# First attention: both score matmuls interleaved in two halves of the TensorE array, and later keys zeroed after the exponential

## The chip, the cores and the metric

One core of one Trainium2 chip. The metric is the device time of one execution in microseconds (us), the median of three runs.

## The reference

Two layers run on a stream of 16 sequences of 256 tokens with 128 channels: attention, experts, a second attention with fixed offsets, and experts with a capacity. The change lies in the first attention:

```python
q = apply_rope(q) * scale          # (16, 16 heads, 256, 8)
k = apply_rope(k)
dots = jnp.einsum('bnih,bnjh->bnij', q, k)
i = jnp.arange(l)
mask = i[:, None] < i[None, :]
dots = jnp.where(mask, jnp.float32(-100000.0), dots)
attn = jax.nn.softmax(dots, axis=-1)
o = jnp.einsum('bnij,bnjh->bnih', attn, v)
return o.transpose(0, 2, 1, 3).reshape(b, l, d) @ Wo.T + bo
```

## The kernel before

`attention0` is a pipeline over the 16 batches. On every engine one function, `run`, takes a list of steps written by hand, each with a stage letter, and issues the list once per repeat b. The letter tells which batch the step works on: L is b+4 (layer norm), A b+3 (projections, rotation, split), S b+2 (values, last part, loads), M b+1 and N b+2 (maxima of the scores), C b (exponentials and outputs), D b−1 (division, projection out, residual). Every engine works through its own list strictly in order; semaphores tie them together.

Scores must be as exact as float32, but are computed from bfloat16 terms. GpSimd adds the two halves of the rotation (`split_parts`, L403) and splits the sum into three bfloat16 parts (L407, L409, L411 and, as `last_part`, L417). SP stores the parts to DRAM in six transfers (L364, L367) and loads them back (L370) with the six products of parts as 48 rows (8 channels by 6 terms) under `qs` and `ks`, for all heads. Both have three buffers, one per batch in flight.

From these TensorE computes the scores twice. `scores_m(g, n)` has queries on partitions and keys along the row; VectorE takes each row's maximum (`maxima`, L672). `scores_c(g, n)` has keys on partitions and queries along the row. Three further rows of `qs` there hold the negated maximum in three parts (L382, L384), so that ScalarE's exponential (`exps`, L437) needs nothing more. Heads go in four groups g, and each group in three units n: units 0 and 1 are two heads of 256 columns, unit 2 is four heads of 128. Each unit fills one PSUM bank: first a matmul of the identity with a mask (`causal`, L472), which puts −1e30 where the key is later than the query, then the score matmuls on top of it (L488, L495 for c; L513, L520 for m). `outputs(g)` multiplies the exponentials `pr` (two buffers, by g) with the values (L546, L548), once the group's three exponentials are done.

The steps that the prediction speaks of, in TensorE's list: `project(1)` (L568) gives the keys' projection of batch b+3, which `rotate(1)` on VectorE (L649, L651) turns and GpSimd splits; `scores_m(0, 0)` of stage N is the first use of batch b+2's loads, and waits for `spread`, the semaphore of both loads; `turn_normal` is L592, `turn_max` L532, `project_out` L598. `statistics` (L625 to L632) on VectorE precedes GpSimd's `rstd_of` (L395, L397), and `normalise` (L638) follows it.

GpSimd's list is short:

```python
run(pool, [("S", last_part), ("A", split_parts), ("L", rstd_of)])
```

## Time and profile before

| | us |
|---|---|
| median of 3 runs | 1368.03 |
| lowest, highest | 1363.39, 1371.96 |
| the profiled execution, its time | 1355.89 |
| its span in the trace | 1354.0 |
| first attention in the span | about 0 to 445 |
| TensorE, VectorE, ScalarE, GpSimd busy in the span | 82%, 60%, 36%, 22% |
| mean granted TensorE clock | 0.882 of full speed |

Full speed of TensorE's clock is 2.4 GHz and its lower level 1.2 GHz. Matmuls are pipelined, so what one costs is read from the distance of two starts, not from its duration. A row of several instructions (x4) is a merged stretch. An arrow in brackets names what an idle time ended with. VectorE is DVE, ScalarE ACT, GpSimd POOL, and SP issues all DMAs of this stage.

### The profile page before, as it was taken

The page shows a single profiled execution, that of the slowest core. Times are in us where ns is not written, and L with a number is a line of the kernel's source. Part 1 is how long each engine was busy: PE and PEld are TensorE (multiplying, and loading weights), DVE is VectorE, ACT ScalarE, POOL GpSimd, SP SyncE. Part 2 cuts the span into 40 slices and gives each one's busy share as a digit, 9 for nine tenths or more (in the row PEclk, how much of TensorE's full clock was granted, in tenths as well). Part 3 has the DMA queues.
Part 4 walks back from the last instruction along what each step waited for, and adds up shares of the span by engine and source line. Part 5 has one row for each costly group of instructions (what it writes and reads, how often), then busy time and mean ns, then how long its engine had stood idle before and what let it go on. Part 6 is the DMA issues. An engine that isn't in the chain of part 4 may idle for free. (4 is left out here: it accounts for less than half of the span.)

```text
span 1354.0 us, 25150 instructions
## 1 busy us (share of the span) xinstructions
PE 1105.7 (82%) x9345; PEld 654.5 (48%) x9345; DVE 815.0 (60%) x1910; ACT 483.5 (36%) x839; POOL 298.3 (22%) x283
## 2 busy tenths in 40 slices
PE   3699999999999599999999996588888889845140
PEld 2235454544444244444444442376777667744130
DVE  4456666646552466566666653488888888646322
ACT  0024444424445133323323321455555564411020
POOL 4132323213210000000000002342332321015536
PEclk9969999959999699999999998589999999855575
DMA  4534242422420622321332230323223322040233
GB/s 128 143 97 96 51 95 49 94 48 49 96 51 3 230 80 94 104 90 63 124 96 95 62 126 0 111 80 97 78 68 96 96 65 81 1 125 26 71 105 85
DMA packets 83989, 113.38 MB, mean 84 GB/s; under 512 B 9658, under 2 KB 53616, under 8 KB 81664
## 3 DMA queue, kind: packets, MB, share of 16 engines
q1 hardware_dynamic: 81840, 108.65, 28.5%
q0 software_dynamic: 2048, 3.37, 0.9%
q8 instruction: 64, 1.05, 0.3%
q14 instruction: 37, 0.30, 0.1%
HBM read 80.18 MB, written 32.65 MB: 83 GB/s over the span
## 5 line engine op out<-in xcount | busy, mean ns | idle before, releaser
L672 DVE TENSOR_REDUCE a_nmax<-ps 128x2 f32<-128x512 f32 (+1 forms) x192 | 132.4, 691 | 127.7 <-PE ps L513 88.2
L437 ACT ACTIVATE a_pr<-ps 128x512 f32<-128x512 f32 x192 | 114.2, 597 | 173.9 <-PE ps L488 124.9
L861 ACT ACTIVATE e_sg<-ps 128x512 f32<-128x512 f32 x136 | 81.2, 597 | 244.6 <-PE ps L886 231.5
L1050 DVE TENSOR_TENSOR e_up<-e_sg,ps 128x512 f32<-128x512 f32 x128 | 88.0, 687 | 106.9 <-PE ps L893 100.9
L886 PE MATMUL ps<-e_hT,e_wg 128*128 128x512 f32 x272 | 140.8, 600 | 0.8 <-DVE e_wT L1037 0.8
L902 PE MATMUL ps<-e_hm,e_wd 128*128 128x512 f32 x272 | 139.2, 594 | 1.4 <-DVE e_hm L1053 0.7
L472 PE MATMUL ps<-a_mask,identb 128*128 128x256 bf16 (+1 forms) x384 | 129.1, 336 | 13.5 <-DMA a_ks<-a_terms_d 9.4
L893 PE MATMUL ps<-e_hT,e_wu 128*128 128x512 f32 x272 | 139.8, 596 | 0.0
L1053 DVE TENSOR_TENSOR e_hm<-e_up,e_wb 128x512 f32<-128x512 f32 x128 | 88.5, 692 | 5.6
L902 PEld LDWEIGHTS ps<-e_hm,e_wd 128*128 128x128 f32 x272 | 51.5, 190 | 67.3 <-issue 63.5
L893 PEld LDWEIGHTS ps<-e_hT,e_wu 128*128 128x128 f32 x272 | 52.1, 191 | 65.6 <-issue 59.8
L1581 POOL TENSOR_TENSOR a_prod<-a_q,a_kp 128x768 f32<-128x768 f32 (+1 forms) x32 | 53.3, 1688 | 131.8 <-PE ps L1789 128.3
L886 PEld LDWEIGHTS ps<-e_hT,e_wg 128*128 128x128 f32 x272 | 50.0, 193 | 53.0 <-issue 51.7
L472 PEld LDWEIGHTS ps<-a_mask,identb 128*128 128x128 bf16 x384 | 38.1, 99 | 70.3 <-issue 38.4
L403 POOL TENSOR_TENSOR a_ra<-a_ra,a_rb 128x512 f32<-128x512 f32 x16 | 20.2, 1262 | 235.4 <-DVE a_rb L651 235.4
L837 POOL TENSOR_TENSOR e_rstd<-e_mv,eps 128x4 f32<-128x4 f32 x8 | 1.6, 199 | 290.2 <-DVE e_mv L964 290.2
L1861 DVE TENSOR_TENSOR a_lg<-ps,a_gw 128x1024 f32<-128x1024 f32 x32 | 59.0, 1886 | 9.9 <-PE ps L1768 8.3
L513 PE MATMUL ps<-a_ks,a_qs 48*128 48x256 bf16 x256 | 54.5, 297 | 0.0
L488 PE MATMUL ps<-a_qs,a_ks 51*128 51x256 bf16 x256 | 52.5, 287 | 0.0
L1882 DVE TENSOR_TENSOR a_lg<-a_lg,a_bias 128x2208 f32<-128x2208 f32 x16 | 49.3, 3079 | 2.1 <-DVE a_lg L1872 0.5
L1571 POOL TENSOR_TENSOR a_rstd<-a_mv,eps 128x2 f32<-128x2 f32 x16 | 30.7, 1920 | 72.9 <-DVE a_mv L1845 72.9
L1621 ACT ACTIVATE a_pT<-ps 128x512 f32<-128x512 f32 x64 | 34.4, 597 | 32.2 <-PE ps L1672 32.2
(266 smaller groups left out, 2031.6 us busy)
## 6 DMA issues: line engine op xcount, KB each, us to landing
e_wb<-e_wT_d SPq DMA_DIRECT2D x128, 256.0 KB, 3.3
a_gw<-a_gd_d SPq DMA_DIRECT2D x16, 1024.0 KB, 5.0
a_gd_d<-a_gc SPq DMA_DIRECT2D x64, 132.0 KB, 2.3
a_terms_d<-a_parts SPq DMA_DIRECT2D x32, 192.0 KB, 2.1
a_qs<-a_terms_d SPq DMA_DIRECT2D x16, 384.0 KB, 5.0
a_ks<-a_terms_d SPq DMA_DIRECT2D x16, 384.0 KB, 6.0
a_terms_d<-a_parts SPq DMA_DIRECT2D x32, 128.0 KB, 2.1
a_terms_d<-a_parts SPq DMA_DIRECT2D x32, 64.0 KB, 1.8
```

Of the source, the lines that this page charges most:

```text
L437: nc.scalar.activation(dst, src, ACT.Exp).then_inc(exp_done, 1)
L472: nc.tensor.matmul(out, identb[:], mask[:, form, 0:n], start=True, stop=False, skip_group_check=True)
L513: mm = nc.tensor.matmul(blocks[:, a], qs[0:ROWS, p, h, P:L], ks[0:ROWS, p, h, :], start=False, stop=(a == 1), skip_group_check=True)
L672: nc.vector.tensor_reduce(dst, src, AX_X, ALU.max, negate=True).then_inc(m_read, 1)
L861: nc.scalar.activation(sg[:, par], ps[:, 2 + par], ACT.Silu).then_inc(silu_done, 1)
L886: nc.tensor.matmul(ps[:, 2 + par, :], wg[:, u, :], hT[:, b.k % 2, :], start=True, stop=True).then_inc(gates_full, 1)
L893: nc.tensor.matmul(ps[:, 4 + par, :], wu[:, u, :], hT[:, b.k % 2, :], start=True, stop=True).then_inc(ups_full, 1)
L902: nc.tensor.matmul(ps[:, 0, :], wd[:, u, :], hm[:, (b.k + u) % 2, :], start=(u == 0), stop=(u == UNITS - 1), skip_group_check=True).then_i ...
L1050: nc.vector.tensor_tensor(up[:, par], sg[:, par], ps[:, 4 + par], ALU.mult).then_inc(up_done, 1)
L1053: nc.vector.tensor_tensor(hm[:, par], up[:, par], wb[:, (u - 1) % RING], ALU.mult).then_inc(hidden_done, 1)
L1581: m = nc.gpsimd.tensor_tensor(prod[:, s0:s0 + n, :], q[:, b.k % 2].unsqueeze(1).to_broadcast([P, n, L]), bass.AP(tensor=a.tensor, offset=a ...
L1861: n = nc.vector.tensor_tensor(lg[:, k, :, 0:WIN].rearrange("p (r j) n -> p r j n", j=HG), ps[:, 0:HJ, k * L:(k + 1) * L].rearrange("p r (j ...
```

## The change

In the first attention:
- The terms are loaded twice into each of `qs` and `ks`: once from row 0, once from row 64 (`M_ROW`). `spread` counts four loads a batch.
- `scores_m` reads rows 64 to 111, `scores_c` rows 0 to 50. A new step `scores` opens both units and then alternates their matmuls: c, m, c, m.
- `scores_c` has no mask matmul any more. Instead the exponentials of later keys are set to zero: in the first 128 queries' blocks by VectorE (`keep_near`, a minimum with 0 or 1e30, twice a group), in the last 128 by GpSimd (`keep_far`, an affine_select once a group, behind a product of one element). `outputs` waits for both.
- GpSimd's `split_parts` is cut in two around one `keep_far`. The lists of TensorE, VectorE and GpSimd are written anew.

In the last stage, four semaphores are merged into two, with no other effect on the order of its work.

```diff
-    masks = np.stack([np.tile(later[:, None], (1, 4, 1)), np.tile(later.T[:, None], (1, 4, 1))], 1)
+    keep = np.where(q > k, 0.0, -NEG).astype(np.float32)
+    masks = np.stack([np.tile(later[:, None], (1, 4, 1)), np.tile(keep[:, None], (1, 4, 1))], 1)
...
-        STORE, SPREAD = 16 * len(RUNS), 16 * 2
+        STORE, SPREAD = 16 * len(RUNS), 16 * 4
...
-                    sp.dma_start(dst[0:ROWS, b.k % 3].rearrange("p h n -> p (h n)"),
-                                 terms_d[side].rearrange("t (d h) n -> (t d) (h n)", h=H)).then_inc(spread, 16)
+                    for row in (M_ROW, 0):
+                        sp.dma_start(dst[row:row + ROWS, b.k % 3].rearrange("p h n -> p (h n)"),
+                                     terms_d[side].rearrange("t (d h) n -> (t d) (h n)", h=H)).then_inc(spread, 16)
...
+            def keep_far(g):
+                def step(b):
+
+                    pool.wait_ge(exp_done, b.x * UN + 3 * g + 3)
+                    hold(pool, far_kept, HG, b, g)
+                    own = pr[:, g % 2, :, L:L + P]
+                    nc.gpsimd.tensor_tensor(pause[:], unit[:], unit[:], ALU.mult)
+                    nc.gpsimd.affine_select(own, own, [[0, HJ], [1, P]], ALU.is_ge, 0.0, base=0, channel_multiplier=-1
+                                            ).then_inc(far_kept, 1)
+                return step
...
-            run(pool, [("S", last_part), ("A", split_parts), ("L", rstd_of)])
+            run(pool, [("S", last_part), ("C", keep_far(0)), ("A", split_parts), ("C", keep_far(1)), ("A", split_rest),
+                       ("L", rstd_of), ("C", keep_far(2)), ("C", keep_far(3))])
...
+            def score_c(g, n, a, b):
+
+                p, bank = b.k % 3, ps[:, 2 + (3 * g + n) % 2]
+                h = HG * ((2 * n if n < 2 else 0) + a) + g
+                out = bank.rearrange("p (a n) -> p a n", a=count_of(n))[:, a]
+                mm = nc.tensor.matmul(out, ks[0:TOP + 3, p, h, 0:P] if n < 2 else ks[0:TOP + 3, p, h, P:L],
+                                      qs[0:TOP + 3, p, h, :] if n < 2 else qs[0:TOP + 3, p, h, P:L],
+                                      start=True, stop=True, skip_group_check=True)
...
+            def score_m(g, n, a, b):
...
+                mm = nc.tensor.matmul(out, qs[M_ROW:M_ROW + ROWS, p, h, P:L] if n < 2 else qs[M_ROW:M_ROW + ROWS, p, h, 0:P],
+                                      ks[M_ROW:M_ROW + ROWS, p, h, :] if n < 2 else ks[M_ROW:M_ROW + ROWS, p, h, 0:P],
+                                      start=False, stop=(a == count_of(n) - 1), skip_group_check=True,
+                                      tile_position=(M_ROW, 0))
...
+                    if has_c:
+                        open_c(g, n)(b)
+                    if has_m:
+                        open_m(gm, n)(m)
+                    for a in range(count_of(n)):
+                        if has_c:
+                            score_c(g, n, a, b)
+                        if has_m:
+                            score_m(gm, n, a, m)
...
-                    pe.wait_ge(exp_done, b.x * UN + 3 * g + 3)
+                    pe.wait_ge(near_kept, b.x * 2 * HG + 2 * g + 2)
+                    pe.wait_ge(far_kept, b.x * HG + g + 1)
...
+            def keep_near(g, n):
+                def step(b):
+
+                    v.wait_ge(exp_done, b.x * UN + 3 * g + n + 1)
+                    own = pr[:, g % 2, 2 * n:2 * n + 2, 0:P]
+                    nc.vector.tensor_tensor(own, own, keep[:, 0:2], ALU.min).then_inc(near_kept, 1)
+                return step
...
-            run(v, [("M", maxima(2, 0)), ("M", maxima(2, 1)), ("M", maxima(2, 2)), ("S", values),
+            run(v, [("M", maxima(2, 0)), ("M", maxima(2, 1)), ("C", keep_near(0, 0)), ("M", maxima(2, 2)),
+                    ("C", keep_near(0, 1)), ("S", values), ("M", maxima(3, 0)), ("D", divide(0)), ("M", maxima(3, 1)),
```

How the instructions now follow each other is seen at two places. The first is GpSimd, one repeat from the second step of the split to the last part of the next batch. `a_parts` and `a_ra` are the split, `a_rstd` the layer norm, `a_pr` the exponentials. Before:

```order
L407 TENSOR_TENSOR a_parts<-a_ra,a_unit 128x2x256
L409 TENSOR_TENSOR a_ra<-a_ra,a_parts 128x512
L411 TENSOR_TENSOR a_parts<-a_ra,a_unit 128x2x256
L395 TENSOR_TENSOR a_rstd<-a_mv,eps 128x2
L397 TENSOR_TENSOR a_rstd<-a_rstd,pm 128x2
L417 TENSOR_TENSOR a_parts<-a_ra,a_parts 128x2x256
```

After, the same stretch:

```order
L414 TENSOR_TENSOR a_parts<-a_ra,a_unit 128x2x256
L428 TENSOR_TENSOR a_pause<-a_unit 128x1
L429 AFFINE_SELECT a_pr<-a_pr 128x4x128
L418 TENSOR_TENSOR a_ra<-a_ra,a_parts 128x512
L420 TENSOR_TENSOR a_parts<-a_ra,a_unit 128x2x256
L402 TENSOR_TENSOR a_rstd<-a_mv,eps 128x2
L404 TENSOR_TENSOR a_rstd<-a_rstd,pm 128x2
L428 TENSOR_TENSOR a_pause<-a_unit 128x1
L429 AFFINE_SELECT a_pr<-a_pr 128x4x128
L428 TENSOR_TENSOR a_pause<-a_unit 128x1
L429 AFFINE_SELECT a_pr<-a_pr 128x4x128
L437 TENSOR_TENSOR a_parts<-a_ra,a_parts 128x2x256
```

Three selects now stand between the split's second step and the last part, the two last of them directly ahead of it.

The second is TensorE, from turn_normal (`a_on`) to the scores' second unit of stage N. `a_hT` is a projection, `a_nbits` turn_max, `a_mask` a mask matmul. Before:

```order
L592 MATMUL ps<-ident,a_on 128x128 x2
L472 MATMUL ps<-a_mask,identb 128x2x128
L513 MATMUL ps<-a_ks,a_qs 128x256 x2
L568 MATMUL ps<-a_hT,a_w 128x256 x2
L472 MATMUL ps<-a_mask,identb 128x2x128
L488 MATMUL ps<-a_qs,a_ks 128x256 x2
L532 MATMUL ps<-identb,a_nbits 48x128 x2
L472 MATMUL ps<-a_mask,identb 128x2x128
L513 MATMUL ps<-a_ks,a_qs 128x256 x2
```

After:

```order
L630 MATMUL ps<-ident,a_on 128x128 x2
L493 MATMUL ps<-a_mask,identb 128x2x128
L526 MATMUL ps<-a_qs,a_ks 128x256
L537 MATMUL ps<-a_ks,a_qs 128x256
L526 MATMUL ps<-a_qs,a_ks 128x256
L537 MATMUL ps<-a_ks,a_qs 128x256
L606 MATMUL ps<-a_hT,a_w 128x256 x2
L569 MATMUL ps<-identb,a_nbits 48x128 x2
L493 MATMUL ps<-a_mask,identb 128x2x128
L526 MATMUL ps<-a_qs,a_ks 128x256
L537 MATMUL ps<-a_ks,a_qs 128x256
```

One mask matmul opens each pair, and the exponent unit (L526) that stood alone now runs within the pair; the first of these pairs is the first to read the newly loaded batch.

## Rows read from the trace of the kernel before

**Rows 1.** Windows: start:end, length, busy PE, PEld, DVE, ACT, POOL (count), clock, DMA.

```profile
200.00:240.00 40.00, 38.92 (x321) 19.87 (x319) 25.25 (x66) 17.45 (x33) 13.05 (x14) 1.00 0.26 54
```

**Rows 2.** Timeline of GpSimd: start, us, instruction; ends at last batch's L403.

```profile
95.55 1.26 POOL L403 TENSOR_TENSOR a_ra<-a_ra,a_rb 128x512 f32<-128x512 f32 x1 [19.29 <-DVE a_rb L651]
...
207.22 1.26 POOL L403 TENSOR_TENSOR a_ra<-a_ra,a_rb 128x512 f32<-128x512 f32 x1 [13.93 <-DVE a_rb L651]
...
209.82 1.15 POOL L409 TENSOR_TENSOR a_ra<-a_ra,a_parts 128x512 f32<-128x512 f32 x1
...
213.59 0.19 POOL L395 TENSOR_TENSOR a_rstd<-a_mv,eps 128x2 f32<-128x2 f32 x1 [1.50 <-DVE a_mv L632]
...
214.54 1.16 POOL L417 TENSOR_TENSOR a_parts<-a_ra,a_parts 128x512 bf16<-128x512 f32 x1
229.68 1.26 POOL L403 TENSOR_TENSOR a_ra<-a_ra,a_rb 128x512 f32<-128x512 f32 x1 [13.98 <-DVE a_rb L651]
...
377.46 1.26 POOL L403 TENSOR_TENSOR a_ra<-a_ra,a_rb 128x512 f32<-128x512 f32 x1 [14.30 <-DVE a_rb L651]
```

**Rows 3.** Timeline of TensorE's matmuls in the steady stretch.

```profile
215.10 0.28 PE L472 MATMUL ps<-a_mask,identb 128*128 128x256 bf16 x1
215.31 0.39 PE L488 MATMUL ps<-a_qs,a_ks 51*128 51x256 bf16 x2
215.63 0.28 PE L472 MATMUL ps<-a_mask,identb 128*128 128x256 bf16 x1
...
217.24 0.39 PE L472 MATMUL ps<-a_mask,identb 128*128 128x512 bf16 x1
...
217.89 0.39 PE L472 MATMUL ps<-a_mask,identb 128*128 128x512 bf16 x1
...
227.03 0.27 PE L472 MATMUL ps<-a_mask,identb 128*128 128x256 bf16 x1
...
227.56 1.13 PE L568 MATMUL ps<-a_hT,a_w 128*128 128x256 f32 x4
...
231.71 0.66 PE L546 MATMUL ps<-a_pr,a_vv 128*32 128x256 f32 x8
...
233.06 0.27 PE L472 MATMUL ps<-a_mask,identb 128*128 128x256 bf16 x1
```

**Rows 4.** Timeline of SP's DMA issues for one batch's two loads.

```profile
218.86 0.36 SPq L370 DMA_DIRECT2D a_qs<-a_terms_d  x1
220.07 0.32 SPq L370 DMA_DIRECT2D a_ks<-a_terms_d  x1
```

**Rows 5.** DMA issues in 214.6 to 226.8 us: count, size, us to landing.

```profile
a_qs<-a_terms_d SPq DMA_DIRECT2D x1, 384.0 KB, 5.3
a_ks<-a_terms_d SPq DMA_DIRECT2D x1, 384.0 KB, 6.2
```

**Rows 6.** Timeline of TensorE in the second attention: four row groups.

```profile
892.75 0.53 PE L1716 MATMUL ps<-a_emb,a_q 32*128 32x152 f32 x7 [1.15 <-ACT a_kp L1605]
```

**Rows 7.** The tile e_zero: min, median and max ns, first and last start.

```profile
L833 POOL MEMSET e_zero<- x1: 956/956/956, 445.0 to 445.0; 128x1024 f32 x1
```

**Rows 8.** Timeline of VectorE in the same repeat.

```profile
211.76 0.69 DVE L672 TENSOR_REDUCE a_nmax<-ps 128x2 f32<-128x512 f32 x1 [1.71 <-PE ps L513]
...
214.00 0.41 DVE L714 TENSOR_TENSOR x<-x,ps 128x256 f32 x1
...
215.00 1.04 DVE L638 TENSOR_SCALAR a_y<-x,a_mv,a_rstd 128x128 f32 x2
```

**Rows 9.** Timeline of ScalarE: one exponential.

```profile
213.75 0.60 ACT L437 ACTIVATE a_pr<-ps 128x512 f32<-128x512 f32 x1 [0.85 <-PE ps L495]
```

**Rows 10.** Windows as in rows 1; the last two numbers are DMA share and GB/s.

```profile
64.00:68.00 4.00, 2.63 (x7) 1.40 (x7) 0.79 (x2) 0.00 (x0) 0.00 (x0) 0.67 0.97 392
221.00:223.00 2.00, 2.00 (x14) 1.02 (x13) 1.63 (x6) 0.72 (x2) 0.00 (x0) 1.00 1.01 152
```

**Rows 11.** Timeline of TensorE in the prologue, after a wait for a DMA.

```profile
42.71 0.40 PE L472 MATMUL ps<-a_mask,identb 128*128 128x256 bf16 x1 [6.02 <-DMA a_ks<-a_terms_d]
...
43.58 2.07 PE L568 MATMUL ps<-a_hT,a_w 128*128 128x256 f32 x4
```

More of the change, by code:

```diff
@@ L214, in _ @@
             nc.vector.tensor_scalar(a0["sinq"][:], a0["sink"][:], a0["scale"][:], None, ALU.mult)
-            nc.vector.tensor_copy(a0["mask"][:], a0["maskf"][:])
+            nc.vector.tensor_copy(a0["mask"][:], a0["maskf"][:, 0])
             for layer in range(2):
@@ L301, in attention0 @@
         cosk, sink = s["a0_w"]["cosk"], s["a0_w"]["sink"]
-        mask, gabo = s["a0_w"]["mask"], s["a0_w"]["gabo"]
+        mask, keep, gabo = s["a0_w"]["mask"], s["a0_w"]["maskf"][:, 1], s["a0_w"]["gabo"]
         vv, ks = s["a0_w"]["vv"], s["a0_w"]["ks"]
@@ L320, in attention0 @@
         yo = sb("yo", [P, L])
-        unit = sb("unit", [P, 1])
+        unit, pause = sb("unit", [P, 1]), sb("pause", [P, 1])
         terms_d = nc.dram_tensor("a0_terms_d", [2, len(TERMS), P, L], BF16).ap()
@@ L351, in body @@
                 for stage, step in order:
+                    if stage == "B":
+                        step(b)
+                        continue
                     c = b + ahead[stage]
@@ L469, in _, with causal, open_c @@
         def _(pe):
-            def causal(out, form, n):
-                nc.tensor.matmul(out, identb[:], mask[:, form, 0:n], start=True, stop=False, skip_group_check=True)
-            def scores_c(g, n):
+            def causal(out, n):
+                nc.tensor.matmul(out, identb[:], mask[:, 0:n], start=True, stop=False, skip_group_check=True)
+            def open_c(g, n):
                 def step(b):
-                    p = b.k % 3
                     if g == 0 and n == 0:
@@ L480, in step, with open_m @@
                     hold(pe, exp_done, UN, b, 3 * g + n - 1)
-                    bank = ps[:, 2 + (3 * g + n) % 2]
-                    if n < 2:
-                        blocks = bank.rearrange("p (j n) -> p j n", j=2)
-                        causal(blocks[:, :, 0:P], 1, 2)
-                        for a in range(2):
-                            h = HG * (2 * n + a) + g
-                            mm = nc.tensor.matmul(blocks[:, a], ks[:, p, h, 0:P], qs[:, p, h, :],
-                                                  start=False, stop=(a == 1), skip_group_check=True)
-                    else:
-                        blocks = bank.rearrange("p (j n) -> p j n", j=HJ)
-                        causal(blocks, 1, HJ)
-                        for j in range(HJ):
-                            h = HG * j + g
-                            mm = nc.tensor.matmul(blocks[:, j], ks[:, p, h, P:L], qs[:, p, h, P:L],
-                                                  start=False, stop=(j == HJ - 1), skip_group_check=True)
-                    mm.then_inc(c_full, 1)
                 return step
-            def scores_m(g, n):
+            def open_m(g, n):
                 def step(b):
-                    p = b.k % 3
                     if g == 0 and n == 0:
@@ L507, in step @@
                     if n < 2:
-                        blocks = bank.rearrange("p (j n) -> p j n", j=2)
-                        causal(blocks[:, :, P:L], 0, 2)
-                        for a in range(2):
-                            h = HG * (2 * n + a) + g
-                            mm = nc.tensor.matmul(blocks[:, a], qs[0:ROWS, p, h, P:L], ks[0:ROWS, p, h, :],
-                                                  start=False, stop=(a == 1), skip_group_check=True)
-                    else:
-                        blocks = bank.rearrange("p (j n) -> p j n", j=HJ)
-                        causal(blocks, 0, HJ)
-                        for j in range(HJ):
-                            h = HG * j + g
-                            mm = nc.tensor.matmul(blocks[:, j], qs[0:ROWS, p, h, 0:P], ks[0:ROWS, p, h, 0:P],
-                                                  start=False, stop=(j == HJ - 1), skip_group_check=True)
@@ new lines, in scores @@
+            def scores(g, n, stage, gm):
+                ahead = {"M": 1, "N": 2}[stage]
+                def step(b):
+                    m = b + ahead
+                    has_c, has_m = 0 <= b.k < B, 0 <= m.k < B
+                    if has_c:
[7 more added lines that the diff above has]
+                            score_m(gm, n, a, m)
@@ L673, in maxima, with step @@
                 return step
+            def keep_near(g, n):
+                def step(b):
+                    v.wait_ge(exp_done, b.x * UN + 3 * g + n + 1)
+                    own = pr[:, g % 2, 2 * n:2 * n + 2, 0:P]
+                    nc.vector.tensor_tensor(own, own, keep[:, 0:2], ALU.min).then_inc(near_kept, 1)
+                return step
             def nmaxes(b):
```

67 lines of the change are left out of this document (40 added, 27 removed).

## The prediction

> **What bounds the kernel now.** I read the windows first, then the first attention's steady repeat on one engine after the other in order of time, then the queue of DMAs. In the window of [rows 1] TensorE is busy 38.92 of 40 us at the full clock. All other engines have room: VectorE 25.25, ScalarE 17.45, GpSimd 13.05. The stage repeats every 22.46 us: L403, GpSimd's first step of a batch, starts at 207.22 and again at 229.68 [rows 2]. TensorE's share of that closes. A score unit with 256 columns is a mask matmul (215.31 − 215.10 = 0.21 us) and two score matmuls (215.63 − 215.31 = 0.32), together 0.53; one with four blocks takes 217.89 − 217.24 = 0.65 [rows 3]. A batch has 16 of the first and 8 of the second: 13.7 us. The other 8.8 us are projections, transposes and outputs with one short wait.
>
> There is a second loop which no wait shows, because it is a little shorter. TensorE's maximum scores of the batch two ahead (their mask matmul at 227.03 [rows 3]) need that batch's two loads. The loads need the parts stored, the stores need GpSimd's L417, and L417 comes behind the GpSimd work of the repeat before. I cut the loop in two:
> - From those scores to L417. L417 starts at 214.54 [rows 2], and the scores one repeat earlier at 227.03 − 22.46 = 204.57: 9.97 us.
> - From L417 to the landed loads. The load of ks is issued at 220.07 [rows 4] and lands 6.2 us later [rows 5], at 226.27: 11.73 us.
>
> Together 21.7 us against a repeat of 22.46. Only 0.76 us of slack are left, and the change works on both halves.
>
> **TensorE: what goes.** The 12 exponent units lose their masks, and a unit of each kind runs interleaved, one in rows 0 to 50 and one from row 64. If the two halves overlap, a pair costs 0.53 or 0.65 in place of twice that: 8 × 0.53 + 4 × 0.65 = 6.8 us in place of 13.7. If they do not, the second unit's matmuls add at least the columns' time, some 0.21 a pair, 12 × 0.21 = 2.5 us. That row groups can overlap is visible here: L1716 has K = 32 in four row groups, and seven matmuls of 152 columns lie in 0.53 us [rows 6], where four full ones of 256 columns take 1.13 us at the same clock (L568 at 227.56, [rows 3]): 0.28 us each for 1.7 times the columns, so seven in a row would be 1.17 us. I take overlap. TensorE's own work falls to about 15 us a repeat. Alone that would be worth 6.9 us × 16 batches = 110 us; it can be had only if nothing else is late next. The second loop is.
>
> **GpSimd: what comes onto the loop.** Four affine_selects on 128x512 and four tiny products. The trace has no affine_select. From below, writing 1024 elements takes 0.96 us [rows 7], so 512 take 0.48. From above, a tensor_tensor of that size takes 1.26 (L403, [rows 2]), twice that if it must wait for VectorE each time, 2.5. I take 1.06, near the L409 and L403 rows (1.15 and 1.26) less the second operand, with 0.19 for the tiny product (L395): 1.25 us. The new GpSimd order puts one select between L414 and L418 and two ahead of the last part. From the scores (time 0) the first half of the loop now is:
> - L403's start at 229.68 − 227.03 = 2.65 [rows 2, 3], L403 and L407 209.82 − 207.22 = 2.60, the select of group 1: 6.5 us. TensorE's outputs of group 1 wait for this; its own work got there at about 4.2.
> - outputs and project_out 233.06 − 231.71 = 1.35 [rows 3], a score pair 0.53, some 0.15 to the semaphore: VectorE starts the maxima of group 1 at 8.55. GpSimd's L418 and L420 lie beside this.
> - From there to GpSimd's rstd takes 213.59 − 211.76 = 1.83 [rows 2, 8], and rstd to L417 214.54 − 213.59 = 0.95: 11.35 us.
> - Two selects, groups 2 and 3: 13.85 us. The exponentials that they wait for are 0.60 us each [rows 9] and done before.
>
> So 13.85 us in place of 9.97. With a select of 0.48 it is 12.1, with 2.5 it is 18.
>
> **SP: what comes onto the loop.** Four loads of 384 KB in place of two, in one queue; the next stage waits for all four. Now qs lands at 218.86 + 5.3 = 224.16 and ks at 226.27 [rows 4, 5], 2.11 us behind it. Two more of that kind: 11.73 + 4.2 = 15.95 us. From below: if the copies into the upper rows run beside the others, only issue time is added, 2 × 0.36 = 0.7. From above: at 152 GB/s [rows 10] two loads of 393 KB take 5.2. That the queue is full is in [rows 10] too: all DMA engines are busy in 221 to 223 us at only 152 GB/s into 48 rows, while loads that fill 128 rows ran at 392. So the limit there seems to lie at the rows written, and it could be that rows from 64 up have a limit of their own.
> The Trainium skill (SBUF — State Buffer, "Can I just issue two DMAs to hit both halves?") speaks against that hope: two transfers, one at partition 0 and one at partition 64, gained only 6% over a single one, they serialize. By this page the loads add about 4 us, as the sum has it; its section on the port swizzle, read alone, would promise that the two halves use different ports and so the rival below. No run here shows either yet.
>
> **VectorE.** Eight minima on 256 elements a batch. The nearest row reads 256 elements from PSUM, 0.41 us [rows 8]; 8 × 0.41 = 3.3 us, in an engine with 37% free. Below 0.3 each would be the columns alone; above, a wait for GpSimd: L638's two operations take 1.04 us at 215.00, although the pair's second ends 0.34 us behind L417's end at 215.70 [rows 2, 8]. So up to 1.2 us more each. They wait beside the DMA chain, which is the longer one; I count nothing.
> The Trainium skill (SBUF — State Buffer, "Who interferes with whom") says that a VectorE instruction with two SBUF inputs contends with a GpSimd instruction that reads SBUF, and one of the two fully blocks. By it each minimum and each select may hold the other up. The row of L638 agrees for another kind of operation; no row shows a minimum.
>
> **The sum.** The loop is 13.85 + 15.95 = 29.8 us at the full clock. TensorE has work for 15 of it, so it stands for the other half, most of that ahead of the scores. After a wait of 6.02 us in the prologue its matmuls ran at half rate: L568 took 2.07 us at 43.58 in place of 1.13 [rows 3, 11], the 1.2 GHz level. With that level the TensorE steps on the path (0.53 + 0.96 at its start, 1.35, 0.53) double: 33.2 us. I take the middle, 31.5 us. Before, the repeats from 95.55 to 377.46 [rows 2] are 12 of 23.5 us, with their own slower stretches. Stage N runs in repeats 0 to 13 with stage C beside it, so thirteen intervals are governed by the loop: 13 × (31.5 − 23.5) = +104 us. The first two batches have no exponents yet but load twice as much: 2 × 4.2 = +8. The last two batches load nothing and gain TensorE's saving in part: −8, of a possible −14. Sum +104 us on the profiled execution's 1355.9 (span 1354.0): 1460. The median of the three runs, 1368.0, lies 12 above it; on it I predict 1472 us. The change in the last stage only merges semaphores and moves nothing: 0.
>
> **Rivals.**
> 1. The halves load beside each other (20%). For it: 152 against 392 GB/s. Against it: one queue, in which qs and ks already land one after the other. The loop is 13.85 + 12.4 = 26.3, with some lower clock 27.5: 13 × 4 + 1 − 8 = +45, so 1413 us.
> 2. The selects or the minima block each other (8%). For it L638, against it that the selects mostly fall into VectorE's free time. With 2.5 us a select the loop is 18 + 16 = 34, with the clock 35.5: 13 × 12 = +156, so 1524 us.
> 3. Not slower (8%, half of it faster by over 1%): selects at 0.48 us and loads in parallel for no more than their issue. Then 12.1 shrinks further, since TensorE's outputs are no longer held (to about 10.6), and the loop is 10.6 + 11.9 = 22.5, the repeat of the fast stretches. The time is then 13 × (22.5 − 23.5) − 8 = −21: 1347 us. It decides from a loop of 23.5 us on, and both conditions are needed.
> 4. The score matmuls do not overlap: TensorE needs 17.5 us in place of 15, still under every loop above. It changes no number here.
>
> **Chances.** Forecast 64%, rivals 20, 8 and 8. A measurement of this kernel tells about 1% from no change. Faster by over 1% 0.04, within 1% 0.05, slower 0.91. The forecast's own range is 1440 to 1505 us (both clock levels throughout, loads at 2.1 to 2.6). For eight in ten it has to reach into the first rival below and toward the second above: 1395 to 1515 us.
>
> **What would show it.** Right: a repeat of about 31 us between starts of L410; TensorE's longest wait is for a DMA into ks, at the mask matmul (L493) behind turn_normal; ks's last load lands some 10 us behind the first issue; three selects lie between rotate's end and L437; the granted clock falls below 1 in these stretches. Wrong: a repeat under 24 us, or TensorE waiting for VectorE or GpSimd more than for DMA, or the four loads landing within 7 us of the first issue.

## The result, and the profile after

| | us |
|---|---|
| the changed kernel, median of 4 runs | 1474.8 (1467.76 to 1482.89) |
| the kernel before beside it, median of 4 runs | 1369.99 |
| ratio, 95% interval | 1.077 (1.070 to 1.084) |
| the profiled execution after, span | 1476.33, 1474.6 |
| first attention in the span | about 0 to 563 (before: 445) |
| mean granted TensorE clock | 0.802 (before: 0.882) |

The change makes the kernel slower by 7.7%; 1472 us were predicted. Some executions of any kernel fall in a slower state of the chip; medians here are over all executions, ratios over those outside it. The page's busy times after: TensorE has fewer matmuls to do (9153, before 9345) and more time to do them in.

```profile
PE 1081.1 (73%) x9153; PEld 637.6 (43%) x9153; DVE 857.1 (58%) x2038; ACT 482.3 (33%) x839; POOL 365.2 (25%) x411
```

The window that answers to [rows 1], of the changed kernel (start:end, length, busy PE, PEld, DVE, ACT, POOL, clock, DMA share, GB/s):

```profile
200.00:240.00 40.00, 27.33 (x204) 12.53 (x204) 19.88 (x51) 11.68 (x22) 15.60 (x21) 0.63 0.31 62
```

TensorE was busy for 38.92 of these 40 us and is now busy for 27.33, at a clock of 0.63. What it waits for is in its timeline (answers to [rows 3]):

```profile
262.58 0.39 PE L493 MATMUL ps<-a_mask,identb 128*128 128x256 bf16 x1 [7.08 <-DMA a_ks<-a_terms_d]
262.90 0.39 PE L526 MATMUL ps<-a_qs,a_ks 51*128 51x256 bf16 x1
262.91 0.39 PE L537 MATMUL ps<-a_ks,a_qs 48*128 48x256 bf16 x1
263.09 0.42 PE L526 MATMUL ps<-a_qs,a_ks 51*128 51x256 bf16 x1
263.09 0.42 PE L537 MATMUL ps<-a_ks,a_qs 48*128 48x256 bf16 x1
263.44 2.08 PE L606 MATMUL ps<-a_hT,a_w 128*128 128x256 f32 x4
...
270.01 1.10 PE L584 MATMUL ps<-a_pr,a_vv 128*32 128x256 f32 x8 [1.16 <-POOL a_pr L429]
...
294.26 0.39 PE L493 MATMUL ps<-a_mask,identb 128*128 128x256 bf16 x1 [5.84 <-DMA a_ks<-a_terms_d]
```

The first pair that reads a new batch waits 7.08 and 5.84 us for the load of ks. L526 and L537 start within 0.01 us of each other: the two halves of the array do work at once. The four projections behind (L606) take 2.08 us in place of the 1.13 of [rows 3], the 1.2 GHz level. GpSimd in the same repeat (answers to [rows 2]):

```profile
106.32 1.26 POOL L410 TENSOR_TENSOR a_ra<-a_ra,a_rb 128x512 f32<-128x512 f32 x1 [14.10 <-DVE a_rb L689]
...
266.52 1.26 POOL L410 TENSOR_TENSOR a_ra<-a_ra,a_rb 128x512 f32<-128x512 f32 x1 [15.59 <-DVE a_rb L689]
268.00 1.04 POOL L414 TENSOR_TENSOR a_parts<-a_ra,a_unit 128x512 bf16<-128x512 f32 x1 [0.22 <-POOL a_ra L410]
269.00 0.37 POOL L428 TENSOR_TENSOR a_pause<-a_unit 128x1 f32<-128x1 f32 x1
269.32 0.63 POOL L429 TENSOR_SCALAR_AFFINE_SELECT a_pr<-a_pr 128x512 f32<-128x512 f32 x1
269.93 1.34 POOL L418 TENSOR_TENSOR a_ra<-a_ra,a_parts 128x512 f32<-128x512 f32 x1
...
275.34 0.20 POOL L402 TENSOR_TENSOR a_rstd<-a_mv,eps 128x2 f32<-128x2 f32 x1 [2.95 <-DVE a_mv L670]
...
276.30 0.19 POOL L428 TENSOR_TENSOR a_pause<-a_unit 128x1 f32<-128x1 f32 x1
276.44 0.63 POOL L429 TENSOR_SCALAR_AFFINE_SELECT a_pr<-a_pr 128x512 f32<-128x512 f32 x1
277.15 0.33 POOL L428 TENSOR_TENSOR a_pause<-a_unit 128x1 f32<-128x1 f32 x1
277.44 0.75 POOL L429 TENSOR_SCALAR_AFFINE_SELECT a_pr<-a_pr 128x512 f32<-128x512 f32 x1
278.16 1.15 POOL L437 TENSOR_TENSOR a_parts<-a_ra,a_parts 128x512 bf16<-128x512 f32 x1
...
489.83 1.26 POOL L410 TENSOR_TENSOR a_ra<-a_ra,a_rb 128x512 f32<-128x512 f32 x1 [15.91 <-DVE a_rb L689]
```

From 106.32 to 489.83 are 12 repeats of 31.96 us (before: 12 of 23.5). The scores start at 262.58 and L437 at 278.16: 15.58 us. From there to the next scores at 294.26 are 16.10 us. SP's issues in between, and how long the loads take to land:

```profile
279.33 1.44 SPq L370 DMA_DIRECT2D a_terms_d<-a_parts  x3
280.81 1.52 SPq L373 DMA_DIRECT2D a_terms_d<-a_parts  x3
282.47 0.83 SPq L377 DMA_DIRECT2D a_qs<-a_terms_d  x2
283.67 0.77 SPq L377 DMA_DIRECT2D a_ks<-a_terms_d  x2
```

```profile
a_qs<-a_terms_d SPq DMA_DIRECT2D x2, 384.0 KB, 5.8
a_ks<-a_terms_d SPq DMA_DIRECT2D x2, 384.0 KB, 9.2
```

The landing is a median over the two loads of a buffer: 9.2 us where one load of ks took 6.2 [rows 5].

### The profile page after: what moved, and what is told of

The parts are those of the page before. It is cut to its first block and busy times, and to the rows that moved or that the text cites. A ratio compares the mean times of both kernels' runs of the same rounds, so it can differ in the third digit from the quotient of the medians.

```text
span 1474.6 us, 25339 instructions
## 1 busy us (share of the span) xinstructions
PE 1081.1 (73%) x9153; PEld 637.6 (43%) x9153; DVE 857.1 (58%) x2038; ACT 482.3 (33%) x839; POOL 365.2 (25%) x411
## 5 line engine op out<-in xcount | busy, mean ns | idle before, releaser
L493 PE MATMUL ps<-a_mask,identb 128*128 128x256 bf16 (+1 forms) x192 | 80.9, 421 | 108.6 <-DMA a_ks<-a_terms_d 73.3
L537 PE MATMUL ps<-a_ks,a_qs 48*128 48x256 bf16 (+1 forms) x512 | 103.3, 320 | 0.0
L526 PE MATMUL ps<-a_qs,a_ks 51*128 51x256 bf16 (+1 forms) x512 | 99.4, 312 | 1.8 <-ACT a_pr L458 1.3
L1628 POOL TENSOR_TENSOR a_prod<-a_q,a_kp 128x768 f32<-128x768 f32 (+1 forms) x32 | 60.0, 1895 | 135.5 <-PE ps L1836 132.0
L493 PEld LDWEIGHTS ps<-a_mask,identb 128*128 128x128 bf16 x192 | 21.0, 110 | 152.1 <-issue 116.1
L584 PE MATMUL ps<-a_pr,a_vv 128*32 128x256 f32 x512 | 58.5, 530 | 34.3 <-POOL a_pr L429 25.9
L410 POOL TENSOR_TENSOR a_ra<-a_ra,a_rb 128x512 f32<-128x512 f32 x16 | 20.2, 1262 | 247.8 <-DVE a_rb L689 247.8
L718 DVE TENSOR_TENSOR a_pr<-a_pr,a_maskf 128x256 f32<-128x256 f32 x128 | 60.2, 470 | 8.5 <-ACT a_pr L458 8.4
L526 PEld LDWEIGHTS ps<-a_qs,a_ks 51*128 51x128 bf16 x512 | 34.2, 107 | 59.8 <-issue 55.3
```

The lines of the kernel that those rows point to most:

```text
L493: nc.tensor.matmul(out, identb[:], mask[:, 0:n], start=True, stop=False, skip_group_check=True)
L526: mm = nc.tensor.matmul(out, ks[0:TOP + 3, p, h, 0:P] if n < 2 else ks[0:TOP + 3, p, h, P:L], qs[0:TOP + 3, p, h, :] if n < 2 else qs[0:TO ...
L537: mm = nc.tensor.matmul(out, qs[M_ROW:M_ROW + ROWS, p, h, P:L] if n < 2 else qs[M_ROW:M_ROW + ROWS, p, h, 0:P], ks[M_ROW:M_ROW + ROWS, p, ...
L718: nc.vector.tensor_tensor(own, own, keep[:, 0:2], ALU.min).then_inc(near_kept, 1)
```

## The experiments

Each ran beside the kernel before, whose median was 1354.9 to 1368.4 us from one set of runs to the next; so the ratio says more than the difference. A repeat is the distance of two starts of GpSimd's first step of a batch, and an average goes over 12 of them unless it says otherwise.

**One load per buffer (e1).** In the changed kernel:

```diff
+                        if row == 0 or b.k < 3:
                             sp.dma_start(dst[row:row + ROWS, b.k % 3]...
...
```

> The changed kernel with the loads into rows from 64 on issued for the first three batches only (one load per buffer from then on; the maxima of later batches come from old terms, which the kernel leaves out of the computation). Theory (the loop from the scores over GpSimd's last part and the loads back to the scores sets the repeat; four loads stand in one queue): from L437 to the scores 16.1 us fall to about 11.7, the repeat from 32.0 to about 27.5 us, 13 repeats times 4.4 and 8 us of the first batches: 1475 - 65 = about 1410 us. Rival A (the halves load beside each other and cost only their issue): 1475 - 13 x 1 = about 1460 us. Rival B (GpSimd and VectorE blocking each other or TensorE's work set the repeat): no change, 1475 us.

Measured: 1400.6 us, ratio 1.030 (1.022 to 1.039). The repeat is 26.0 us (102.02 to 414.14 in 12), 6.0 less than after: 11.5 us from the last part to the scores (L440 at 243.67, scores at 255.20) in place of 16.1, and 14.6 in the first half (scores at 229.09), one less than after, with the clock at 0.74. The second load costs 4.6 us behind the last part, where the sum has 4.2; with it the first half is 1 us longer too, at a lower clock. Rivals A and B fall.

**One load of 128 rows, first try (e2).** The source is given as a copy of two with stride zero in front:

```diff
+                    sp.dma_start(dst[:, b.k % 3].rearrange("p h n -> p (h n)"),
+                                 terms_d[side].rearrange("t (d h) n -> (t d) (h n)", h=H).unsqueeze(0)
+                                 .to_broadcast([2, P // 2, H * L])).then_inc(spread, 16)
...
```

> The changed kernel with one load of 128 rows per buffer in place of two of 48 rows: the terms in DRAM are padded with two terms of ones and read twice, 1 MB a load. Theory (the loads stand in one queue, and what a load costs is set by the rows it writes at once and not by its bytes): 1 MB at the 392 GB/s of rows 10 is 2.7 us in place of 2 x 2.1, so the last lands about 3 us sooner, the repeat is about 29 us, and the time 1475 - 13 x 3 - 6 = about 1430 us. Rival (the 152 to 164 GB/s of these loads is a limit of the path and holds for wide loads too): 6.6 us a load, 13.2 for both in place of 8.4, the repeat 37 us, about 1540 us.

Measured: 1976.2 us, ratio 1.455. Neither the theory nor the rival held; a repeat takes 62 us. The window of a stretch in which nothing but such a load runs:

```profile
300.00:320.00 20.00, 0.00 (x0) 0.00 (x0) 0.00 (x0) 0.00 (x0) 0.00 (x0) 0.50 0.13 53
```

The DMA share is 0.13, which is that of 2 of 16 engines. That fits the Trainium skill (DMA: Bandwidth & Descriptors, "Rules for kernel authors"): a leading dimension of two copies confines the whole transfer to at most two DMA engines. The run told nothing on the rows, and was repeated in another form:

**One load of 128 rows, contiguous (e11).** Each part is stored twice, beside two terms of ones:

```diff
+        terms_d = nc.dram_tensor("a0_terms_d", [2, 2, 8, P, L], BF16).ap()
...
+                    for c in range(2):
+                        sp.dma_start(terms_d[0, c, n:n + m]...
...
+                                 terms_d[side].rearrange("c t (d h) n -> (c t d) (h n)", h=H)).then_inc(spread, 16)
```

> The changed kernel with the terms stored twice (twelve stores a batch in place of six) beside two terms of ones, so that one load of 128 contiguous rows, 1 MB, fills a buffer. It repeats e2_wide_load with a transfer that all 16 DMA engines can share. Theory (a load that writes 128 rows runs at the 392 GB/s of rows 10): 2.7 us a load in place of 2 x 2.1, but the stores take some 3 us longer: repeat 31 to 32.5 us, about 1475 us, with windows at 350 GB/s or more. Rival (some 150 GB/s is a limit of these DRAM rows whatever they are written to): 6.6 us a load, repeat 39 us, about 1565 us.

Measured: 1468.4 us, ratio 1.079 (1.070 to 1.087), repeat 31.2 us (103.24 to 477.16). A window of 3 us within such a load, and the landings of both buffers' loads between 217 and 226 us:

```profile
221.50:224.50 3.00, 0.00 (x0) 0.00 (x0) 0.00 (x0) 0.00 (x0) 0.00 (x0) 1.00 0.96 404
```

```profile
a_qs<-a_terms_d SPq DMA_DIRECT2D x1, 1024.0 KB, 5.0
a_ks<-a_terms_d SPq DMA_DIRECT2D x1, 1024.0 KB, 6.3
```

1 MB into 128 rows lands in 5.0 and 6.3 us, as fast as 384 KB into 48 rows did [rows 5]. The same 16 engines move 404 GB/s; two windows of the changed kernel in which only loads into 48 rows run have less than half of that:

```profile
288.00:290.00 2.00, 0.41 (x3) 0.17 (x2) 0.99 (x4) 0.00 (x0) 0.00 (x0) 1.00 0.95 160
290.00:292.00 2.00, 0.00 (x0) 0.00 (x0) 0.00 (x0) 0.00 (x0) 0.00 (x0) 1.00 1.01 172
```

Both kinds of load move packets of 8 KB, so the size of the packets is not the difference: the median packet takes 0.81 us in the changed kernel (285 to 291 us) and 0.31 us here (221.5 to 224.5 us). At 8 KB a row, a load of 48 rows costs as much as one of 128. The stores eat what this saves, as expected: from the start of the last part to the first load are 8.3 us in place of 4.3 (209.51 to 217.80, against 278.16 to 282.47), and from there to the scores 7.5 in place of 11.8.

**A second queue for the upper rows (e5).** ScalarE issues the two loads from row 64 on, behind its fifth exponential:

```diff
+                    nc.scalar.dma_start(dst[M_ROW:M_ROW + ROWS, b.k % 3].rearrange("p h n -> p (h n)"),
...
```

> The changed kernel with the two loads into rows from 64 on issued by ScalarE, in a queue of its own, beside SP's loads from row 0. Theory (the 16 DMA engines, all busy at some 150 GB/s while such loads run, are the limit, and a second queue only shares them): the last of the four loads lands as late as before, within 1 us, the repeat stays at 31 to 32 us, about 1470 us. Rival (one queue makes them stand in line): two loads run beside two, the last lands some 4 us sooner, the repeat is about 28 us, 1475 - 13 x 4 = about 1423 us.

Measured: 1479.3 us, ratio 1.093 (1.085 to 1.100), repeat 32.0 us. Windows while loads of the two queues are under way (in the first one SP's are, and ScalarE's begin at 249.25):

```profile
248.00:250.00 2.00, 2.00 (x25) 1.13 (x24) 2.00 (x8) 1.19 (x2) 0.00 (x0) 1.00 1.16 197
250.00:252.00 2.00, 1.43 (x22) 0.86 (x20) 1.84 (x7) 1.05 (x2) 0.00 (x0) 1.00 1.01 147
252.00:254.00 2.00, 1.35 (x6) 0.96 (x6) 0.93 (x4) 0.00 (x0) 0.00 (x0) 1.00 1.01 164
```

Two queues move no more than one did: 147 to 197 GB/s here, 160 and 172 in the windows above, with all engines busy. In the repeat read, the upper loads were issued at 249.25 and 249.60, three us behind the first lower one. A load of ks by itself lands in 6.2 us [rows 5]; ScalarE's took 9.0. The next scores started at 258.72, 16.8 us behind the last part; in the changed kernel it was 16.1. The rival falls. The Trainium skill (SBUF — State Buffer, "Can I just issue two DMAs to hit both halves?") says just that: they serialize, and other issuing engines do not help.

**The last part ahead of rstd and of the last select (e3).**

```diff
-            run(pool, [("S", last_part), ("C", keep_far(0)), ("A", split_parts), ("C", keep_far(1)), ("A", split_rest),
-                       ("L", rstd_of), ("C", keep_far(2)), ("C", keep_far(3))])
+            run(pool, [("C", keep_far(0)), ("A", split_parts), ("C", keep_far(1)), ("A", split_rest),
+                       ("C", keep_far(2)), ("A", last_part), ("L", rstd_of), ("C", keep_far(3))])
```

> The changed kernel with GpSimd's last part moved ahead of the layer norm's rstd and of the select of group 3; everything else stays. Theory (the loop): the stores start at the end of the select of group 2, about 273.7 in place of 278.2 in the repeat read, so the first half of the loop falls from 15.6 to about 11.2 us, the repeat from 32.0 to 27.6, the time to 1475 - 13 x 4.4 = about 1418 us. Rival A (GpSimd's order is not on the path, the DMAs alone are): 1475 us. Rival B (rstd, now later, holds the layer norm and the next projections): some of it comes back, 1440 us.

Measured: 1442.3 us, ratio 1.060 (1.048 to 1.071), repeat 28.9 us: a gain of 3.0 us in place of 4.4. GpSimd's timeline names what the expectation left out:

```profile
252.21 0.64 POOL L429 TENSOR_SCALAR_AFFINE_SELECT a_pr<-a_pr 128x512 f32<-128x512 f32 x1
254.82 1.17 POOL L437 TENSOR_TENSOR a_parts<-a_ra,a_parts 128x512 bf16<-128x512 f32 x1 [1.97 <-PE ps L526]
```

The last part now waits 1.97 us for an exponent unit, 30.1 us in 12 such waits between 100 and 440 us. With three buffers a batch is loaded where the current batch's terms stand, so `last_part` holds until that batch's last unit. It is a second edge of the loop. Rival B's number (1440 us) is met, but hardly by its mechanism: in the same stretch VectorE's layer norm (L676) waits for the later rstd 7.9 us in all, at most 0.9 at a time.

**No zeroing at all (e6).**

```diff
-                    pe.wait_ge(near_kept, b.x * 2 * HG + 2 * g + 2)
-                    pe.wait_ge(far_kept, b.x * HG + g + 1)
+                    pe.wait_ge(exp_done, b.x * UN + 3 * g + 3)
...
+            run(pool, [("S", last_part), ("A", split_parts), ("A", split_rest), ("L", rstd_of)])
```

> The changed kernel without the minima on VectorE and without the selects and the tiny products on GpSimd; outputs waits for the exponentials alone. Later keys then count in the sums, which the kernel leaves out of the computation. Theory (the selects stand on the loop): the one between L414 and L418 costs 0.9 us, the two ahead of the last part 1.8, TensorE's waits for them in outputs(1) 1.2; with VectorE free sooner the first half falls from 15.6 to about 12 us, the repeat from 32 to about 28.3, 1475 - 13 x 3.7 = about 1427 us. Rival A (they hide beside the loads): no change, 1475 us. Rival B (they alone make the change slow, the loads being hidden): back to the 23.5 us of before, about 1365 us.

Measured: 1425.5 us, ratio 1.056 (1.046 to 1.066), repeat 28.2 us (103.47 to 442.15). The forecast was 1427 and 28.3. Both halves of the loop are thus confirmed one by one: without the second load the repeat is 6.0 us shorter, without the zeroing 3.7. The two together are more than the 8.5 us between the two kernels, since each also gives back some of the clock (0.71 and 0.74 over 100 to 380 us, where the changed kernel has 0.66), and TensorE has less work than in the kernel before.

**The kernel before with the loads alone (e4).**

```diff
+                    for row in (64, 0):
+                        sp.dma_start(dst[row:row + ROWS, b.k % 3].rearrange("p h n -> p (h n)"),
...
```

> The kernel before with one part of the change alone: each buffer is loaded a second time, into rows from 64 on, which nothing reads. Theory (the loop had 0.8 us of slack and the loads stand in one queue): 9.97 + 15.95 = 25.9 us in place of 23.5, with a little lower clock 26.5, so 13 x 2.4 to 13 x 3 and 8 us of the first batches: +39 to +47, about 1370 + 43 = 1413 us. Rival A (the halves load beside each other): loop 22.5, 1370 us. Rival B (the loads alone cost nothing since the loop is no bound in the kernel before): 1370 us, with ks landing 4 us later all the same.

Measured: 1447.4 us, ratio 1.065 (1.051 to 1.079): more than twice the 43 us expected. Two repeats of it as windows:

```profile
219.00:244.00 25.00, 22.08 (x183) 11.29 (x183) 14.13 (x37) 9.80 (x19) 6.55 (x7) 1.00 0.45 96
...
273.80:309.30 35.50, 34.95 (x183) 15.26 (x183) 13.95 (x37) 10.37 (x19) 6.54 (x7) 0.56 0.35 68
```

The first is the loop, 25.0 us where the sum has 25.9. The second has the same 183 matmuls at a clock of 0.56, behind a wait of 3.60 us for ks (at 270.37). TensorE has 22 us of work a repeat at the full clock, and 35 at that level: there the clock makes TensorE the bound. On average a repeat takes 29.3 us (103.93 to 455.00). Rivals A and B fall. That the wait made the clock fall is not shown, for the kernel before has such a repeat too, without a wait for a load:

```profile
274.60:308.45 33.85, 33.31 (x183) 14.86 (x183) 13.97 (x37) 10.03 (x19) 6.55 (x7) 0.60 0.22 48
```

**Halves by batch (e7).** The halves can be filled without a second load: even batches in rows 0 to 50, odd ones in rows 64 to 114, two buffers each.

```diff
+        def at(tile, b, first, n):
+
+            row = 64 * (b.k % 2) + first
+            return tile[row:row + n, b.k // 2 % 2]
...
-                hold(pool, c_full, UN, b + -2, 0)
+                hold(pool, c_full, UN, b + -3, 0)
...
+            run(pe, [("B", pair(0, 0, 2)), ("B", pair(0, 1, 2)), ("B", pair(0, 2, 2)), ("D", outputs(3)), ...
```

> The kernel before with even batches in rows 0 to 50 and odd ones in rows 64 to 114, two buffers each, loaded once, with both mask matmuls on TensorE; the exponent units of groups 0 and 1 alternate with the maximum units of groups 2 and 3 of the next batch, which lie in the other half of the array. Theory (TensorE is the bound by little over the loop): its work falls by 6 x 0.3 us to about 20.2, the loop of 21.7 takes over, so repeats of 21.7 to 22.5 in place of 22.5: 1360 - 13 x 0.5 = about 1353 us, and TensorE waits about 1 us a repeat for the load of ks. Rival (each wait brings the lower clock, and with 20 us of work that costs more than was saved): repeats of 25 us or more, 1385 us.

Measured: 1366.9 us, ratio 1.012 (1.007 to 1.018). Its best repeats in the steady stretch are 21.3 us, the average is 24.5 (92.03 to 385.54), and the clock over 100 to 380 us is 0.84: the rival, in a mild form. With less work TensorE runs into the loop's wait, which the kernel before never did there: between 92 and 385 us it waits for loads of ks 8 times, 11.8 us in all.

**The same with the loop cut (e8).** The projection of the keys and its rotation go ahead of the unit that waits for the loads, in the lists of TensorE and VectorE; in ScalarE's, `take_max` goes one step back:

```diff
-("D", turn_normal), ("N", scores_m(0, 0)), ("A", project(1)), ("C", scores_c(2, 1)), ("M", turn_max), ("N", scores_m(0, 1)), ("C", scores_c(2, 2)), ...
+("D", turn_normal), ("C", scores_c(2, 1)), ("A", project(1)), ("N", scores_m(0, 0)), ("C", scores_c(2, 2)), ("M", turn_max), ("N", scores_m(0, 1)), ...
```

> The kernel of e7_halves_by_batch with the projection of the keys and its rotation moved ahead of the first maximum unit that waits for the loads, so that a late load no longer delays the next batch's loads. Theory (the loop then spans two repeats): a repeat must be at least (20.1 - 1 + 22.8) / 2 = 21.0 us, the slack comes back and the clock stays at its upper level: 13 x 1.5 = 20 us less than before, about 1340 us. Rival (the loop was no bound): as e7.

Measured: 1308.5 us, ratio 0.969 (0.964 to 0.974), faster than both kernels, and 4% below e7, which ran beside the same kernel before. Three repeats as a window:

```profile
235.60:294.80 59.20, 57.40 (x544) 31.08 (x552) 41.31 (x112) 28.82 (x54) 19.57 (x21) 1.00 0.40 84
```

19.7 us a repeat at the full clock, TensorE busy for 97% of it: less than the 21.0 us that the expectation gave as a bound. Its terms were too long. Three rows of TensorE's timeline show how far the real bound is, the projection of the keys (L596, the second of its two stretches), the next, and the unit that waits for the loads (L484):

```profile
253.30 1.13 PE L596 MATMUL ps<-a_hT,a_w 128*128 128x256 f32 x4
...
272.79 1.13 PE L596 MATMUL ps<-a_hT,a_w 128*128 128x256 f32 x4
...
274.11 0.28 PE L484 MATMUL ps<-a_mask,identb 128*128 128x256 bf16 x1 [0.19 <-DMA a_ks<-a_terms_d]
```

From a projection at 253.30 to its loads' landing at 274.11 are 20.8 us, where the expectation had 22.8, and TensorE is busy for 19.1 us a repeat (57.40 / 3), where it had 20.1. With these its form gives (19.1 − 1.3 + 20.8) / 2 = 19.3 us. The next projection now goes 1.3 us ahead of the unit that waits, so no load is waited for once the repeat is 20.8 − 1.3 = 19.5 us, and the wait of 0.19 us says that it stands just there. Between 92 and 385 us the waits for loads are 4 and 1.8 us in all. In the kernel before, the projection stood behind that point, and the loop was the whole chain. One repeat (188.24 to 216.21) takes 28.0 us; TensorE stands still in it for 3.28 and 1.93 us with no releaser that the profile shows, and the clock over it is 0.82. What that is stays open.

**The order alone (e9).** The same three lists in the kernel before, all else unchanged.

> The kernel before with the reordering of e8_halves_reordered alone: rows 0 to 50 only, three buffers, all score units one after the other, but the projection of the keys and its rotation ahead of the first maximum unit that waits for the loads. Theory (TensorE's 22 us a repeat are the bound of the kernel before, the loop only comes close to it): 22.3 us a repeat at the full clock, and the stretches that fall to the lower clock once a load is late become rarer: between 1340 and 1360 us. Rival (the order alone made e8's gain, the halves none): about 1310 us, as e8.

Measured: 1335.3 us, ratio 0.982 (0.974 to 0.990).

```profile
178.60:244.20 65.60, 63.31 (x539) 33.81 (x546) 42.21 (x112) 28.87 (x54) 19.61 (x22) 1.00 0.34 74
```

21.9 us a repeat, and the clock is 1.00 from 92 to 353 us; only one repeat, just ahead of these, is longer (29.1 us, 62.99 to 92.06). But what the order removed here is not a wait for a load. Between 95 and 377 us the kernel before had none; its steady repeats of 22.46 us had this one, which is gone in e9:

```profile
229.66 0.29 PE L532 MATMUL ps<-identb,a_nbits 128*48 128x128 bf16 x2 [0.54 <-DVE a_rb L651]
```

`turn_max` writes the PSUM bank that the projection of the keys was in, and waits for its rotation. In the new order more work stands between the two. That accounts for 0.54 of the 0.61 us by which a steady repeat is shorter. The other two thirds of the 20 us that 12 repeats gain are the slower repeats (33.85 us and 24.02 before), and why e9 has none of them there is not shown. So e9 does not show that the loop through the loads cost the kernel before anything; the pair e7 and e8 shows what it costs once TensorE has less to do.

By the ratios the order is worth 1.8% in the kernel before and 4% with the halves by batch; the halves cost 1.2% without it (e7) and gain 1.3% on top of it. The last is a difference of two sets of runs: by the medians it is 2.0%.

**All parts together (e10)**, with single loads, the loop cut and the change's zeroing:

```diff
-            run(pool, [("S", last_part), ("C", keep_far(0)), ...
+            run(pool, [("C", keep_far(0)), ("A", split_parts), ("C", keep_far(1)), ("A", split_rest), ("A", last_part),
+                       ("L", rstd_of), ("C", keep_far(2)), ("C", keep_far(3))])
```

> Halves by batch (single loads, two buffers in each half), the change's zeroing on VectorE and GpSimd in place of the exponent units' masks, the last part directly behind the split and ahead of the selects, and the projection of the keys ahead of the first pair of the later batch. Theory (off the loop the zeroing is nearly free and TensorE's work falls to about 17 us): a repeat of at least (17 + 21.3) / 2 = 19.2 us, so 19.5 us or as in e8, with some lower clock 20.5: 1300 to 1325 us. Rival (the zeroing delays outputs of every group, each delay opens gaps on TensorE and brings the lower clock): repeats of 22 us and more, 1345 us or above.

Measured: 1381.4 us, ratio 1.015 (1.007 to 1.022); the rival's case, with repeats of 26 us (110.13 to 397.55 in 11). TensorE's waits in this kernel between 100 and 360 us name no load any more, but:

```profile
POOL a_pause L436 <- ACT a_pr L466: 45.3, 21, 4.0
...
PE ps L592 <- POOL a_pr L437: 17.4, 14, 1.7
...
PEld ps L592 <- POOL a_pr L437: 13.1, 10, 1.8
```

GpSimd stands before its selects until an exponential is done, and outputs waits for the selects; the clock is 0.75. So this kernel is slow though no load is waited for. How much of it is the zeroing is not separated: in groups 2 and 3 its pairs, of batches b and b+2, lie in the same half of the array, which e8 does not pair.

**Half of the zeroing (e12)**, VectorE's alone, in e8:

```diff
+                if n == 2:
+                    causal(bank.rearrange("p (j n) -> p j n", j=HJ), 1, HJ)
...
+                    pe.wait_ge(near_kept, b.x * 2 * HG + 2 * g + 2)
```

> The kernel of e8_halves_reordered with half of the change's zeroing: VectorE's minima replace the mask matmuls of the exponent units with 256 columns (8 x 0.21 = 1.7 us of TensorE's work a repeat), the units with four blocks keep theirs, and GpSimd zeroes nothing. Theory (in e10 each zeroing stands in an in-order list between an exponential and outputs, and TensorE waits for it): VectorE's 8 x 0.41 = 3.3 us bring it to 17.4 of 19.4 us, the maxima come later, and waits in outputs and for the maxima take back more than the 1.7 us: repeats of 20 to 21.5 us, 1315 to 1335 us. Rival (only GpSimd's selects cost in e10): TensorE's 17.8 us of work and waits of a few tenths, repeats of 18 to 19 us, 1290 to 1305 us.

Measured: 1308.8 us, ratio 0.960 (0.956 to 0.965); most repeats are 19.5 us. Against e8's 1308.5 and 0.969 no gain can be claimed, since the medians are equal and the intervals of the ratios touch: VectorE is now busy for 83.7 of 100 us (200 to 300 us), TensorE for 92.3. The time lies between theory and rival. With VectorE's minima alone the loss of e10 is gone, which points at GpSimd's selects and their place; but e10 also lacks the masks of the units with four blocks and has another order of pairs, and none of these was tried apart.

## Why the prediction was right, and where its parts were off

**The loop.** It holds: 15.58 + 16.10 = 31.7 us in the repeat read, 31.96 on average, 31.5 predicted. e1, e3, e6 each shorten one part of it and the repeat follows. The signs listed for "right" are there: the repeat, the longest wait at L493 for ks, three selects ahead of L437, a clock below 1; only the last landing comes nearer 12 than 10 us behind the first issue (294.26 − 282.47 = 11.8). There the sign was stated loosely, for the sum itself has 15.95 less the 4.3 us from the last part to the first issue, 11.6.

**GpSimd's half.** Predicted 13.85 at the full clock, measured 15.58. Two terms were off, in opposite directions. Three selects with their products were 3.75 us of it. Measured: the first from 269.00 to 269.95, the last two from 276.30 to 278.16, 2.8 together, so they were taken a third too long. The select's 0.63 us lies near the lower bound (0.48, [rows 7]), not near the L409 row from which I took its 1.06. In return TensorE's steps ran at 1.2 GHz: L410 starts 3.94 us behind the scores where 2.65 were counted, and from the end of group 1's select (269.95) to the maxima of group 1 are 3.56 us where 2.05 were counted:

```profile
273.51 0.69 DVE L710 TENSOR_REDUCE a_nmax<-ps 128x2 f32<-128x512 f32 x1 [3.26 <-PE ps L537]
```

Together that is 2.8 us, near the 3.4 that the sum's upper bound has for the clock. I had half of that bound in the sum by taking a middle (31.5 between 29.8 and 33.2). So the selects were 1 us too much and the clock 1.1 us too little, and that the repeat came out at 31.96 against 31.5 is in part luck.

**The loads.** 15.95 predicted, 16.10 measured. Rival 1, beside each other, is refuted by e5, e1 and e4.

**Blocking.** Rival 2 exists in small:

```profile
268.44 0.88 DVE L718 TENSOR_TENSOR a_pr<-a_pr,a_maskf 128x256 f32<-128x256 f32 x1
...
269.84 0.41 DVE L718 TENSOR_TENSOR a_pr<-a_pr,a_maskf 128x256 f32<-128x256 f32 x1
```

The minimum beside L414 takes 0.88 us, the others of this repeat 0.41 or 0.42, as estimated; and L418, with a minimum at its start, takes 1.34 where [rows 2] has 1.15. Neither is on the loop. The tiny products ahead of the selects of groups 1 and 3 are, and they take 0.37 and 0.33 us with a minimum beside them where that of group 2 takes 0.19: 0.3 us a repeat. The cause is read from the overlap alone; no run tried it apart.

**TensorE.** The halves overlap (L526 and L537 above). The kernel gained nothing by it, as argued: TensorE waits.

**The sum.** The profiled pair differs by 1476.3 − 1355.9 = 120.4 us, where the sum had 104. The stage grew by 562.8 − 445.0 = 117.8: 10.8 up to the first of the repeats counted (95.55 to 106.32; +8 predicted), 101.6 in 12 repeats, 5.4 behind them, where a thirteenth repeat (8.5) and the saving of the last batches fall (−8 predicted; −3 is what is left for it). The medians differ by only 107, from the 1368.0 that the forecast started from. The 12 us that I added for the median belong to the kernel before: the profiled execution after lies 1.5 us above its median. So the sum was 16 us too low and the step to the median 14 us too high, and the hit of 1472 against 1474.8 rests on two errors that cancel: luck as to the last 15 us, not as to the size of the loss.

**Rival 3.** It takes 11.9 us for loads that cost only their issue, where rival 1 has 11.73 + 0.7 = 12.4 for the same. With 12.4 its time would be some 6 us more; the forecast is not touched.

**What the prediction lacked.** It knows the loop only as a limit for what is added, and did not ask how far TensorE's work can be cut before the loop is the bound. That is what e7 and e8 show: with some 2 us less work a repeat for TensorE the kernel gained nothing until the loop was cut, and then 4%.

## What to carry to other kernels

When an engine is nearly full, look for the loop that is just shorter than the repeat, through queues and loads, before giving the engine less to do: work taken off it is worth nothing beyond the loop's slack, and anything added to the loop beyond its slack costs in full, and more where the clock falls. An instruction that waits for a transfer should not stand ahead of the work that feeds the next transfer; with the halves by batch, moving that work ahead was worth 4%, and only then did the freed half of the array pay (3.1% below the kernel before). Two different batches filled the two halves here without a second load; two copies of one batch cost 4.6 us a repeat behind the last part.

## What the runs showed of the hardware

- The same 16 DMA engines, all busy, moved 147 to 197 GB/s into 48 rows (the windows shown) and 404 GB/s into 128 rows, in packets of 8 KB both times: a packet took 0.81 us (median, changed kernel) and 0.31 us (e11). From one queue or from two made no difference (e5).
- A transfer whose leading dimension has two entries ran at a DMA share of 0.13 and 53 GB/s (e2).
- TensorE ran whole repeats at a granted clock of 0.56 to 0.60: 183 matmuls kept it busy for 34.95 us in place of 22.08 (e4), behind a wait of 3.60 us for a load, and for 33.31 us in the kernel before (274.60 to 308.45), with no wait over 0.54 us. For the fuller kernel (22 us of work) doubling the loads cost the loop plus the clock, 29.3 us a repeat for a loop of 25.
- Two matmuls in the two halves of the array (51 rows from 0, 48 rows from 64) start within 0.01 us of each other (changed kernel, L526 and L537).
- affine_select on 128x512 takes 0.63 us on GpSimd; VectorE's minimum of 128x256 with both inputs in SBUF takes 0.41, and 0.88 beside a GpSimd tensor_tensor (changed kernel).
